# A decoder layer on one core: the mean over batches and the choice of lags between two of its stages, rearranged

## The reference

```
x = x + linear_attention(norm(x))          # 16 heads of 8, running sums over positions
x = x + autocorrelation(norm(x), ctx)      # the block around which the change is made
x = x + mixture_of_experts(norm(x))        # 8 experts, the best 2 of each row
```

```
corr       = irfft(rfft(q) * conj(rfft(k)))            # per batch, head and feature: 64 lags
mean_value = corr.mean(over heads and features)        # [128 batches, 64 lags]
index      = top_k(mean_value.mean(over batches), 5)   # 5 lags, the same for all batches
tmp_corr   = softmax(mean_value[:, index])             # per batch, over the 5 lags
out        = sum over the 5 lags of (v rolled by lag) * weight, then @ Wo + bo
```

## Time and profile before

| | |
|---|---|
| median of 3 runs | 722.79 us (722.51 to 724.52) |
| profiled execution: its own time | 719.2 us |
| profiled execution: span from first to last instruction | 717.0 us |
| busy: TensorE, VectorE, GpSimd, ScalarE | 84%, 74%, 61%, 55% of the span |
| mean granted TensorE clock | 0.938 of full speed |
| idle of VectorE ahead of L827 | 4.4 us |
| duration of L827 | 7.0 us, once |
| chain of waits, share of TensorE and VectorE | 40% and 36% |

### The profile page before, as it was taken

The page is one execution under the profiler, slowest core; times in us unless marked ns, Lnnn a source line. Parts: engine busy times, 40 slices in busy tenths (PEclk is TensorE's granted clock), DMA queues, the critical chain, the costliest instruction groups (busy, mean ns, idle before and its releaser), DMA issues.

```text
span 717.0 us, 14240 instructions
## 1 busy us (share of the span) xinstructions
PE 605.7 (84%) x3196; PEld 401.6 (56%) x3197; DVE 528.3 (74%) x1794; ACT 397.4 (55%) x993; POOL 438.3 (61%) x510
## 2 busy tenths in 40 slices
PE   2889999999999998414877754799999999999995
PEld 1445555555555554213766643367666666666663
DVE  4699999999999999362689979566666666656662
ACT  3546566666666664301676632355566666666662
POOL 5999988888888885102344420665266666665662
PEclk9999999999999999955799955799999999999998
DMA  5500111000421111727454310121011111111110
GB/s 148 171 2 0 47 44 30 29 29 29 72 45 30 29 30 47 90 44 234 102 121 120 105 54 15 43 48 44 16 43 46 42 42 45 42 41 41 41 45 19
DMA packets 50609, 40.67 MB, mean 57 GB/s; under 512 B 21827, under 2 KB 40899, under 8 KB 50566
## 3 DMA queue, kind: packets, MB, share of 16 engines
q1 hardware_dynamic: 45574, 29.62, 16.5%
q0 software_dynamic: 4992, 10.56, 5.7%
HBM read 27.29 MB, written 12.88 MB: 56 GB/s over the span
## 4 chain that ended last, share of the span: by engine, by line
PE 40%; DVE 36%; issue 15%; DMA 4%; DVEq 2%; POOL 1%; ACT 1%; SPq 1%; POOLq 0%; ACTq 0%
PE bank L1081 33%; DVE R L731 10%; PE bank L1297 5%; DVE nd L737 4%; DVE st_a L716 2%; DMA ct<-in_ctx_r 2%; DVE st_c L716 2%; DVE st_e L716 1%; DVE X L771 1%; PE bank L1282 1%; DVE best_at L895 1%; DVE rden L750 1%; DVE X L923 1%; DVE den L747 1%; DVE mean_all L827 1%
## 5 line engine op out<-in xcount | busy, mean ns | idle before, releaser
L471 POOL TENSOR_TENSOR shared<-v,qk 128x1152 f32<-128x1152 f32 x64 | 141.0, 2203 | 12.4 <-POOL qk L466 9.4
L1081 PE MATMUL bank<-w_s,shared 128*128 (+1 forms) x312 | 148.3, 598 | 0.1
L1081 PE MATMUL bank<-shared,tri_s 128*128 128x360 f32 (+1 forms) x384 | 136.7, 492 | 5.8 <-DVE R L731 5.4
L525 POOL DMA_INDIRECT shared<-xs_d,row_u x92 | 88.7, 964 | 66.8 <-DVE row_u L991 30.3
L1049 DVE SCALAR_TENSOR_TENSOR hid<-bank,gt,shared 128x256 f32<-128x256 f32 x156 | 75.3, 484 | 47.5 <-ACT shared L675 46.3
L532 POOL DMA_INDIRECT out_x<-shared x64 | 63.1, 987 | 71.5 <-DVE shared L1073 54.1
L731 DVE TENSOR_TENSOR R<-bank,qk 128x360 f32<-128x360 f32 (+1 forms) x192 | 94.8, 547 | 12.5 <-PE bank L1081 10.6
L675 ACT ACTIVATE shared<-bank 128x256 f32<-128x256 f32 x156 | 60.0, 385 | 77.7 <-PE bank L1081 77.7
L1081 PEld LDWEIGHTS bank<-shared,tri_s 128*128 128x128 f32 x384 | 68.7, 191 | 53.1 <-issue 22.6
L737 DVE TENSOR_REDUCE nd<-R 128x144 f32<-128x1152 f32 x64 | 86.6, 1353 | 2.6
L1081 PE MATMUL bank<-w_s,ct 128*128 (+1 forms) x624 | 82.5, 275 | 0.1
(11 more groups left out here) (213 smaller groups left out, 1096.5 us busy)
## 6 DMA issues: line engine op xcount, KB each, us to landing
xs_d<-xs SPq DMA_DIRECT2D x16, 270.0 KB, 3.6
X<-in_x SPq DMA_DIRECT2D x16, 256.0 KB, 2.7
ct<-in_ctx_t SPq DMA_DIRECT2D x16, 256.0 KB, 2.9
gram_d<-gd SPq DMA_DIRECT2D x16, 256.0 KB, 2.4
ct<-in_ctx_r SPq DMA_DIRECT2D x16, 256.0 KB, 3.7
circ<-prob_d SPq DMA_DIRECT2D x32, 64.0 KB, 2.8
w_s<-in_w_up SPq DMA_DIRECT2D x1, 2048.0 KB, 8.7
shared<-xs_d,row_u POOLq DMA_INDIRECT x92, 2.6
```

Of the source, the lines that this page charges most:

```text
L471: nc.gpsimd.tensor_tensor(outer[k], v9[k % 2][:].unsqueeze(3).broadcast_to([P, H, D1, D]), kk.unsqueeze(2).broadcast_to([P, H, D1, D]), AL ...
L525: nc.gpsimd.indirect_dma_start(xg[q], None, xs_d[:, :], bass.IndirectOffsetOnAxis(ap=rows, axis=0)).then_inc(xg_in[q], 16)
L1081: return nc.tensor.matmul(o, l, r, start=start, stop=stop, skip_group_check=True)
```

## The change

The groups 14 and 15 leave `DIAG_PARTS`. The sum over t is made in two pieces. The early one sums batches 0 to 111 on their 112 partitions, as soon as the first two loads have landed, ahead of `split_fold`. The late one sums the 16 last batches, spread over all 128 partitions: each batch has eight partitions, and each of these has 8 of the 64 rows t (512 elements instead of 4096). For that the two last groups are stored to a tensor of their own, `gram_t`, with a batch pitch of 64 times 129 elements, so that one load with a partition step of 8 times 129 gives all of it; the store of a group becomes two stores of 64 partitions each. Two products add both pieces over all batches in `bank[4]`. A third, with a new constant matrix `late_of`, puts the late sums of the eight partitions of a batch on that batch's partition (`bank[3]`), and VectorE adds the early sums. `mean_early` is set to zero at the start by GpSimd, since its last 16 partitions are never written. The division by 128 moves into ScalarE's copy to `gd`; the scale by 1/128 for the mean over batches is dropped, since it doesn't change the order of the lags. The five comparisons become one on [5, 64] elements and a sum over the five. The product with the mask (`masked`) is dropped, and `away` alone masks.

```diff
-DIAG_PARTS = [(0, 8), (8, 14), (14, 16)]
+DIAG_PARTS = [(0, 8), (8, 14)]
+EARLY_B = 2 * GT * DIAG_PARTS[-1][1]
+OCT = P // (B - EARLY_B)
+PITCH = L * (2 * L + 1)
...
+        gram_t = nc.dram_tensor("gram_t", ((B - EARLY_B) * PITCH,), F32).ap()
+        late = w_s[:, L * L:L * L + L // OCT * L].rearrange("p (t l) -> p t l", t=L // OCT)
+        late_of = w_s[:, L * L + L // OCT * L:L * L + L // OCT * L + P]
+        kept_k = w_s[:, 5 * E * NE:5 * E * NE + LAGS * L].rearrange("p (k l) -> p k l", k=LAGS)
...                                                                  # SyncE
-                             (iota_s[:], iota), (dest_s[:], dest), (walk_s[:], walk), (place_s[:], place)):
+                             (iota_s[:], iota), (dest_s[:], dest), (walk_s[:], walk), (place_s[:], place),
+                             (late_of, late_in)):
-            for first, last in DIAG_PARTS[:-1]:
+            for first, last in DIAG_PARTS:
...
             for g in (NG - 2, NG - 1):
-                gram_store(*grp(g))
-            diagonals(*DIAG_PARTS[-1])
+                sp.wait_ge(d_gd, g + 1)
+                for h in range(2):
+                    first_b = (g - DIAG_PARTS[-1][1]) * 2 * GT + h
+                    sp.dma_start(bass.AP(gram_t.tensor, first_b * PITCH, [[2 * L, L], [2 * PITCH, GT], [1, 2 * L]]),
+                                 gd[g % 2][h * L:(h + 1) * L].rearrange("p t a b -> p t (a b)")).then_inc(gram_out[g % 2], 16)
+            for k in range(2):
+                sp.wait_ge(gram_out[k], 16 * (DIAG_PARTS[-1][1] // 2) + 32)
+            sp.dma_start(late, bass.AP(gram_t.tensor, 0, [[PITCH // OCT, P], [2 * L + 1, L // OCT], [1, L]])
+                         ).then_inc(diag_in, 16)
...                                                                  # GpSimd
+            pool.memset(mean_early[:], 0.0).then_inc(early_0, 1)
...                                                                  # ScalarE, the copy to gd
-                                         .unsqueeze(2).broadcast_to([P, GT, 2, L]), ACT.Copy).then_inc(d_gd, 1)
+                                         .unsqueeze(2).broadcast_to([P, GT, 2, L]), ACT.Copy, scale=1.0 / E).then_inc(d_gd, 1)
...                                                                  # VectorE
-            split_fold()
+            dve.wait_ge(early_0, 1)
             dve.wait_ge(diag_in, 16 * len(DIAG_PARTS))
-            mean_step(nc.vector.tensor_reduce(mean_all[:], diag.rearrange("p t l -> p l t"), AX.X, ALU.add))
-            mean_step(nc.vector.tensor_scalar(mean[:], mean_all[:], 1.0 / E, None, ALU.mult))
+            mean_step(nc.vector.tensor_reduce(mean_early[0:EARLY_B], diag[0:EARLY_B].rearrange("p t l -> p l t"), AX.X, ALU.add), False)
+            split_fold()
+            dve.wait_ge(diag_in, 16 * len(DIAG_PARTS) + 16)
+            mean_step(nc.vector.tensor_reduce(mean_late[:], late.rearrange("p t l -> p l t"), AX.X, ALU.add), False)
             dve.wait_ge(mean_mm, 1)
-            mean_step(nc.vector.tensor_scalar(mean_all[:], bank[0][:, 0:L], 1.0 / B, None, ALU.mult))
-            mean_step(nc.vector.max(top8[:], mean_all[:]))
-            mean_step(nc.vector.max_index(top_at[:], top8[:], mean_all[:]))
+            mean_step(nc.vector.max(top8[:], bank[4][:, 0:L]))
+            mean_step(nc.vector.max_index(top_at[:], top8[:], bank[4][:, 0:L]))
             mean_step(nc.vector.tensor_copy(top_f[:], top_at[:]))
-            mean_step(nc.vector.tensor_scalar(kept[0][:], iota_s[:, 0:L], top_f[:, 0:1], None, ALU.is_equal))
-            for k in range(1, LAGS):
-                mean_step(nc.vector.scalar_tensor_tensor(kept[k % 2][:], iota_s[:, 0:L], top_f[:, k:k + 1],
-                                                         kept[(k - 1) % 2][:], ALU.is_equal, ALU.add))
-            keep = kept[(LAGS - 1) % 2]
+            mean_step(nc.vector.tensor_tensor(kept_k, iota_s[:, 0:L].unsqueeze(1).broadcast_to([P, LAGS, L]),
+                                              top_f[:, 0:LAGS].unsqueeze(2).broadcast_to([P, LAGS, L]), ALU.is_equal))
+            mean_step(nc.vector.tensor_reduce(keep[:], kept_k.rearrange("p k l -> p l k"), AX.X, ALU.add))
+            dve.wait_ge(mean_mm, 2)
+            mean_step(nc.vector.tensor_tensor(mean[:], bank[3][:, 0:L], mean_early[:], ALU.add), False)
             mean_step(nc.vector.tensor_scalar(away[:], keep[:], 1.0, 1e30, ALU.subtract, ALU.mult))
-            mean_step(nc.vector.tensor_tensor(masked[:], mean[:], keep[:], ALU.mult))
-            mean_step(nc.vector.tensor_tensor(scores[:], masked[:], away[:], ALU.add))
+            mean_step(nc.vector.tensor_tensor(scores[:], mean[:], away[:], ALU.add))
...                                                                  # TensorE
+            pe.wait_ge(mean_ch, 1)
+            mm(bank[4][:, 0:L], ones_f[:], mean_early[:], True, False)
             pe.wait_ge(mean_ch, MEAN_READY)
-            mm(bank[0][:, 0:L], ones_f[:], mean[:]).then_inc(mean_mm, 1)
-            pe.wait_ge(mean_ch, MEAN_READY + 1)
+            mm(bank[4][:, 0:L], ones_f[:], mean_late[:], False, True).then_inc(mean_mm, 1)
+            mm(bank[3][:, 0:L], late_of, mean_late[:]).then_inc(mean_mm, 1)
```

More of the change, by code:

```diff
@@ L52, in build @@
 def build(nc, x, ctx_t, ctx_r, wqkv_p, b_all, wo, wq2, wk2, wv2t, wo2, bq2, bk2, bv2, scale, w_router, w_up, w_down,
-          tri, stri, ident, iota, dest, walk, place, out):
+          tri, stri, ident, iota, dest, walk, place, late_in, out):
     with ExitStack() as ctx:
@@ L130, in build @@
         gd = [sb(f"gd{i}", [P, GT, 2, L]) for i in range(2)]
-        mean, mean_all = sb("mean", [P, L]), sb("mean_all", [P, L])
+        mean, mean_early, mean_late = (sb(n, [P, L]) for n in ("mean", "mean_early", "mean_late"))
         top8, top_at, top_f = sb("top8", [P, 8]), sb("top_at", [P, 8], U32), sb("top_f", [P, 8])
-        kept = [sb(f"kept{i}", [P, L]) for i in range(2)]
-        away, masked, scores = sb("away", [P, L]), sb("masked", [P, L]), sb("scores", [P, L])
+        keep, away, scores = sb("keep", [P, L]), sb("away", [P, L]), sb("scores", [P, L])
         neg_max, prob, prob_sum, prob_r = sb("neg_max", [P, 1]), sb("prob", [P, L]), sb("prob_sum", [P, 1]), sb("prob_r", [P, 1])
@@ L246, in build @@
         xs_out = sem("xs_out")
+        early_0 = sem("early_0")
         cleared, made, w_scaled = sem("cleared"), sem("made"), sem("w_scaled")
@@ L1343 @@
 PACK_READY = MASK_READY + 3 + PACK
-N_W = 16 * 16
+N_W = 17 * 16
 MEAN_READY = 2
-MEAN_EXP = MEAN_READY + 4 + LAGS + 4
+MEAN_EXP = MEAN_READY + 9
 MEAN_STEPS = MEAN_EXP + 4
 _NAMES = ("x", "ctx_t", "ctx_r", "wqkv_p", "b_all", "wo", "wq2", "wk2", "wv2t", "wo2", "bq2", "bk2", "bv2", "scale",
-          "w_router", "w_up", "w_down", "tri", "stri", "ident", "iota", "dest", "walk", "place")
+          "w_router", "w_up", "w_down", "tri", "stri", "ident", "iota", "dest", "walk", "place", "late_in")
 def _arrays(**v):
@@ L1403, in _arrays @@
         "iota": iota,
+        "late_in": (t == EARLY_B + s // OCT).astype(np.float32),
     }
```

## The result

| | before | changed |
|---|---|---|
| median of 6 runs | 722.72 us (721.87 to 725.08) | 715.66 us (711.79 to 718.04) |
| ratio | | 0.9893 (95% interval 0.9859 to 0.9927) |
| profiled execution: own time, span | 719.2, 717.0 us | 716.84, 715.0 us |
| mean granted clock | 0.938 | 0.934 |

The forecast was 715.6 us in a range of 712.3 to 719.8. The median moved by 7.1 us; the ratio, which is not the quotient of the two medians, is worth 7.7 us. The two profiled executions differ by only 2.0 us of span, and that has to be explained first.

The account below looks back on a forecast made before the run. No single engine was taken to bound the kernel, but a serial chain from the last group's store to neg_max. Terms of 0.33 + 6.2 + 0.26 - 0.06 + 0.42 + 0.04 save 7.2 us: 722.79 to 715.6 us, range 712.3 to 719.8.

Parts of the forecast that it names:

- The stretch: From the last group's store to neg_max: a serial chain, nothing else bounding it; all behind neg_max shifts as a block.
- Its own signs of being wrong: Wrong if late sum starts after 309 us, takes over 1.5 us, or neg_max is 7 us earlier without the end.
- late sum starts earlier: On VectorE behind the late load: the late sum starts at 307.85 instead of 308.18 us, saving 0.33 us.
- sum and scaling: On VectorE: the late sum holds the chain 1.05 us instead of 7.26 with scaling, saving 6.2 us.
- scaling of the mean dropped: Between the late product and the maximum: the dropped scaling step saves 0.26 us.
- maximum and place from PSUM: Search for the maximum and its place: both now read PSUM, costing 0.06 us.
- comparisons: Ahead of neg_max: one comparison and a sum take 1.15 us instead of 1.57, saving 0.42 us.
- rival A: Late load, by ports alone: takes 3.5 us or less, VectorE becomes the later; saved 7.5 us, 715.3 us; chance 18%.
- VectorE's order: Early sum starts at 297.7 us, ahead of split_fold, which ends at 307.45; the late load hides the fold's delay.
- B: Second load needs 2.5 us more, so VectorE's early sum is late; saved 5.0 us, 717.8 us; chance 10%.
- C: Late load needs 10.5 us, late sum starts at 314.05; saved 1.0 us, 721.8 us; chance 5%.
- D: Behind the barrier: the low clock lasts longer; with 25 us more of it the time is 728 us; chance 4%.

Follow-up runs that it names:

- e1: The changed kernel once more, without an edit; 715.62 us, ratio to the kernel before 0.9895.
- e6: The changed kernel with the second half of each late store issued from ScalarE's queue instead of SyncE's; 739.81 us, ratio to the kernel before 0.9933.
- e12: The kernel before once more, without an edit, for a second profile; 746.24 us in one run, on a slower chip.
- e7: The changed kernel with extra products that nothing reads put into TensorE's waits; 742.28 us, ratio to the kernel before 0.9964.
- e4: The changed kernel with split_fold put back ahead of the early sum on VectorE; 719.0 us, ratio to the kernel before 0.9929.
- e5: The kernel before with only the single comparison and sum in place of the five comparisons; 748.94 us, ratio to the kernel before 1.0006.
- e3: The changed kernel with the last 16 batches spread over 64 partitions instead of 128, from the same stores; 716.99 us, ratio to the kernel before 0.9929.
- e9: The changed kernel with extra TensorE products, the last batch of 20 ahead of group 2's value product; 739.56 us, ratio to the kernel before 0.9877.
- e10: The changed kernel with expert weights loaded in eight pairs, their scaling later, and extra products up to group 0's circulants; 735.05 us, ratio to the kernel before 0.9825.
- e11: The changed kernel with expert weights loaded in eight pairs behind the first eight groups and scaled at slot 12; 733.9 us, ratio to the kernel before 0.982.

## Why the prediction was right

*The stretch.* The forecast was that the chain from the last store to `neg_max` is serial, that nothing else bounds it, and that all behind it shifts as a block. The runs bear out all three. From `neg_max` to the first expert product it is 137.86 us in both profiles; that they agree to the hundredth is chance, for the other profiles with nothing edited behind the barrier (e1 to e6, e12) have 136.4 to 138.2.

*Its own signs of being wrong.* The late sum was not to start after 309 us, and `neg_max` was forecast for 312.4. In the first profile they are at 310.61 and 315.09. The prediction counted from the profile of before, whose last copy ends at 300.77, and took that end as given; here the copy ends at 304.05. Counted from the end of the copy the late sum starts after 6.56 us, where the forecast has 7.1, and in e7, whose copy ends at 301.04, it starts at 307.69. So the sign spoke of the clock ahead of the barrier and not of the chain.

*The terms of the sum*, from the profiles of before and after, each from the issue of the last store:

| term | forecast | measured |
|---|---|---|
| late sum starts earlier | 0.33 | 0.78 (7.32 before, 6.54 now) |
| sum and scaling | 6.2 | 6.19 |
| late product | 0 | 0.08 |
| scaling of the mean dropped | 0.26 | 0.26 |
| maximum and place from PSUM | -0.06 | -0.01 |
| comparisons | 0.42 | 0.31 |
| last three steps | 0.04 | 0.12 |
| together | 7.2 | 7.7 |

The first term was mis-sized twice, and the two errors cancel in part; that the sum comes out within 0.5 us is in part luck. The load was forecast at 4.3 us to landing and took 3.3: I took the rate of the 64-partition load, and this is the load of rival A. The pair of stores was forecast to cost 0.2 us more than one and costs 0.7: the late load is issued 3.12 us behind the first store's issue, 2.38 before. I had sized the second store as if half the bytes landed sooner; its landing takes 2.44 us, no less than the 2.31 of the 256 KB, and its issue comes 0.57 + 0.04 later. The comparisons' sum over five took 0.69, the upper of my two rates.

*VectorE's order.* The forecast's end of the fold, 307.45, was 307.25 and 307.65. In e7, where the last group isn't late, the load and the fold end together. That is rival A's case: the load needs less than 3.5 us, and VectorE is no longer idle ahead of the late sum. In the first profile it is idle for 3.36 us, where the forecast had a few tenths, because everything else is 3.3 us late and the early sum is not.

*B and C* didn't occur: the second load landed at 297.4 and the late one needed a third of what C had. B's premise was also misread: for its size the third load is the slowest of the three, 4.84 us for 256 KB, and not the second. *D*: the clock did come back (mean 0.97 from 338 to 400 us, 0.90 before), so there is no slower case. But its mechanism was at work at a place where I had not put it, ahead of the barrier, in both kernels. It moves the end of the last copy by up to 5.4 us in the kernel before; that this is part of the spread of the runs is argued and not shown. The medians, with 7.1 and 8.2 us (e1), are on either side of the 7.7 of the profiles.

*Left open:* the expert stage takes 259.5 us in the first profile of before and 261.7 to 262.9 in the first of the changed kernel and in e1 to e4. Were this the change's doing, the median should have moved by 5 us and not by 7.1 and 8.2; on the two slower chips the kernel before has 282.3 (e12) and, with the new comparison, 283.6 (e5), the kernels with the change 283.3 to 286.4, and e5 and e6 on one chip are 0.3 us apart. A part is the clock: in the first 10 us of this stage TensorE is busy throughout, at a mean granted clock of 0.87 in the profile of before and 0.78 in that of the changed kernel, from which I estimate 0.9 us of the 2.5; e12 has 0.79, so this comes without the change too. On the other side stands e6, the changed kernel but for a queue: its ratio of 0.9933 is worth 5.0 us, its medians 7.5. No run was made for it, so how much of the 7.7 us reaches the end is known to some 2 us only.

## What to carry to other kernels

The reduction here costs what is in one partition, on however many partitions it runs: before taking part of such a step out early, ask on how many partitions the rest lies, and lay the rest across all of them by the pitch of the tensor in memory. The load of small pieces got faster by the same move (4.8 to 3.3 us). Where single profiles disagree with medians, measure the mechanism by the distance between two of its own events: here 10.8 to 11.1 us in the eight profiles that hold the whole change and 18.5 to 18.8 before, while the spans moved by several microseconds for another reason.

## What the runs showed of the hardware that was not expected

- The granted clock falls to 0.5 (1.2 GHz) between 285 and 289 us in eleven of fourteen profiles, of either kernel, while TensorE's work of the first stage runs out (it is busy for 8.46 of 18 us at the high clock); in three it stays high to 302 us or longer. In e1 and e3 it is back at 1.0 by 292 us. The last copy to `gd` ends up to 5.4 us later for it (300.77 and 306.19 in the two profiles of the kernel before).
- Half the bytes in a store land no sooner: 2.4 to 2.9 us for 128 KB, two such stores in a row, and 2.3 us for the last one of 256 KB. A half by itself was not run.
- Extra products in TensorE's waits hold its clock up, but it is at 0.5 again when the chain comes to the value product behind the load of `ct` (e9: 335.9 us), and what they give in the first groups is lost later (e10 against e11).
- On two of the three chips of the experiments all kernels are 3% slower, and it is all in the expert stage: 282 to 286 us from its first product to the end, against 260 to 263 in the profiles of e1 to e4 and the first two.
